# The last block's expert outputs 4 and 5: weighed by ScalarE and added by GpSimd instead of VectorE, with expert 5's matmuls moved earlier on TensorE

## What is computed

```python
x = x + _L0_xattn_ref(_layernorm(x), ctx, mask, ...)      # 16 heads over 77 context rows, with a mask
x = x + _L0_ffn_ref(_layernorm(x), proj_w, anchors, ...)  # 6 experts, the 2 best weighed by a softmax
x = x + _L1_xattn_ref(_layernorm(x), ctx, ctx, ...)       # 16 heads, one key and value head
x = x + _L1_ffn_ref(_layernorm(x), w1, b1, w2, b2)        # 256 -> 1024 -> 256, piecewise gelu
```

```python
h = jax.nn.gelu(jnp.einsum('btd,edh->bteh', x, w1))
out = jnp.einsum('bteh,ehd,bte->btd', h, w2, expert_weights)
```

## Time and profile before

| | us |
|---|---|
| median of 3 executions (793.67 to 794.06) | 793.94 |
| the profiled execution, whole | 797.73 |
| its span, first to last instruction | 795.5 |
| TensorE busy (93% of the span) | 736.2 |
| VectorE busy (82%) | 648.8 |
| ScalarE busy (65%) | 514.5 |
| GpSimd busy (47%) | 371.8 |

### The profile page before, as it was taken

One profiled execution on the slowest core, in us unless ns is written; L12 is line 12 of the kernel. 1 busy time (PEld: TensorE's weight loads), 2 busy tenths in 40 slices (PEclk: granted clock), 3 DMA queues, 4 the chain that ended last, 5 costly groups with the idle time before them and its releaser, 6 DMA issues. The chain is left out here.

```text
span 795.5 us, 13555 instructions
## 1 busy us (share of the span) xinstructions
PE 736.2 (93%) x4372; PEld 552.0 (69%) x4372; DVE 648.8 (82%) x1546; ACT 514.5 (65%) x943; POOL 371.8 (47%) x323
## 2 busy tenths in 40 slices
PE   4799999999999999999989999999869999999995
PEld 3465666666558888888865555555448898888985
DVE  7647777787877878888887888988687999999995
ACT  3545655565654456545536777777677889898985
POOL 6473444334122223233214232232157899999985
PEclk9989999999999999999998999999998999999999
DMA  7985535653310000001057666755000000000001
GB/s 230 133 201 113 131 73 111 119 115 80 77 35 1 1 1 7 1 1 54 1 70 118 83 81 82 134 77 78 13 1 1 2 27 28 28 27 2 27 28 53
DMA packets 25102, 48.64 MB, mean 61 GB/s; under 512 B 3687, under 2 KB 7017, under 8 KB 24521
## 3 DMA queue, kind: packets, MB, share of 16 engines
q1 hardware_dynamic: 23366, 46.54, 30.5%
q10 hardware_dynamic: 1666, 1.24, 0.5%
HBM read 12.12 MB, written 4.19 MB: 21 GB/s over the span
## 5 line engine op out<-in xcount | busy, mean ns | idle before, releaser
L316 ACT ACTIVATE pt<-bank 77x512 f32<-77x512 f32 x256 | 140.8, 589 | 82.7 <-PE bank L416 60.0
L342 DVE TENSOR_REDUCE mx<-bank 128x4 f32<-128x308 f32 x256 | 108.7, 471 | 22.8 <-PE bank L391 12.2
L413 PE MATMUL bank<-qst,l_kst 128*77 128x512 f32 (+1 forms) x256 | 103.2, 418 | 17.0 <-DMA qst<-mt 11.0
L720 POOL TENSOR_TENSOR frise<-fg,fg 128x512 f32<-128x512 f32 x64 | 100.3, 1568 | 6.8 <-ACT fg L738 1.2
L388 PE MATMUL bank<-l_kblk,qh 128*128 128x308 f32 x256 | 81.0, 334 | 7.7 <-DVE mx L342 6.3
L284 POOL TENSOR_TENSOR ol<-ot,oh 128x512 fp32r<-128x512 f32 x32 | 41.4, 1292 | 98.1 <-ACT oh L321 54.6
L617 DVE SCALAR_TENSOR_TENSOR x<-bank,eweight,x 128x256 f32<-128x256 f32 x192 | 79.6, 477 | 4.6 <-PE bank L649 4.3
L103 POOL TENSOR_TENSOR rstd<-var,minus_half 128x4 f32<-128x4 f32 x32 | 34.8, 1088 | 102.7 <-DVE var L98 53.9
L413 PEld LDWEIGHTS bank<-qst,l_kst 128*77 128x77 f32 (+1 forms) x256 | 36.6, 146 | 66.5 <-ACT pt L316 24.8
L811 PE MATMUL bank<-fw2h,fyh 128*128 128x256 f32 x256 | 73.6, 288 | 5.4 <-DVE fyl L779 5.3
L114 ACT ACTIVATE xn<-x,shift,rstd 128x256 f32<-128x256 f32 (+1 forms) x128 | 67.0, 592 | 17.0 <-POOL shift L105 17.0
(11 more groups left out here) (176 smaller groups left out, 2101.1 us busy)
## 6 DMA issues: line engine op xcount, KB each, us to landing
qst<-qh SPq DMA_DIRECT2D x64, 256.0 KB, 6.6
qst<-ql SPq DMA_DIRECT2D x32, 256.0 KB, 9.0
out<-x SPq DMA_DIRECT2D x8, 512.0 KB, 2.6
qst<-ml SPq DMA_DIRECT2D x8, 480.0 KB
x<-in_x SPq DMA_DIRECT2D x3, 1024.0 KB, 12.9
weights<-in_mlp_w SPq DMA_DIRECT2D x2, 1024.0 KB, 5.1
mraw<-in_mask SPq DMA_DIRECT2D x8, 154.0 KB
x<-in_x SPq DMA_DIRECT2D x2, 512.0 KB, 5.5
```

The costliest lines, as they stand in the source:

```text
L316: self.nc.scalar.activation(self.pt[0:T, i // 4 % 2, i % 4, :], self.bank_of(G, i)[0:T, :], ACT.Exp).then_inc(self.probs, 1)
L342: self.nc.vector.reduce_max(out, banks[u % len(banks)][:, 0:4 * T].rearrange("q (p par t) -> q p par t", p=2, par=2), AX.X).then_inc(self. ...
L413: last = self.nc.tensor.matmul(out, layer.kst[rows, layer.stack(c * HC + 2 * k + par), b * T:(b + 1) * T], self.qst[rows, self.slot(G), c ...
L720: self.nc.gpsimd.tensor_tensor(self.rise[:, k % 2, :], self.g1[:, k % self.R, :], self.g0[:, k % self.R, :], ALU.subtract).then_inc(self.r ...
```

## The change

The weighted outputs of experts 4 and 5 of the last block no longer pass through VectorE. ScalarE copies the banks, multiplied by the router's weight, into a new SBUF tile `epart` (`scale_last`: 4 instructions of 128x256 for each expert), and GpSimd adds `epart` to `x` (`add_last`: 2 instructions of 128x512 for each expert). `output` of expert 5 waits for `scaled` instead of `added`, and stands on TensorE between units 5 and 6 of block 8 instead of behind `turn_maxima`. Whoever waited for the last `added` now waits for `last_added` (GpSimd's adds) or, for the bank alone, for `scaled`. The core of the diff:

```diff
+ALL_EXP = 2 * (E * BLOCKS - 2)
...
+        self.part = place.at("epart", m["epart"], [P, 2, NT, D], F32)
...
+    def add_last(self, pool, i):
+
+        pool.wait_ge(self.added, ALL_EXP)
+        start = (BLOCKS - 1) * NT
+        for k in range(2):
+            pool.wait_ge(self.scaled, 2 * i + k + 1)
+            tiles = self.norm.x[:, start + 2 * k:start + 2 * k + 2, :]
+            self.nc.gpsimd.tensor_tensor(tiles, tiles, self.part[:, i, 2 * k:2 * k + 2, :], ALU.add).then_inc(self.last_added, 1)
+            pool.wait_ge(self.last_added, 2 * i + k + 1)
...
+    def scale_last(self, act, i):
+
+        g, e = BLOCKS - 1, 4 + i
+        act.wait_ge(self.weight_ready, BLOCKS)
+        for k in range(2):
+            act.wait_ge(self.out_done, 2 * (E * g + e) + k + 1)
+            for t in range(2):
+                last = self.nc.scalar.activation(self.part[:, i, 2 * k + t, :], self.OUT[k][:, t * D:(t + 1) * D], ACT.Copy,
+                                                 scale=self.weight[:, g % 2, 2 * k + t, e:e + 1])
+            last.then_inc(self.scaled, 1)
...
     def output(self, pe, g, e):
         self.wait_rest(pe, g, e)
         for k in range(2):
-            need(pe, self.added, 2 * (E * g + e - 1) + k + 1)
+            if (g, e) == (BLOCKS - 1, E - 1):
+                pe.wait_ge(self.scaled, k + 1)
+            else:
+                need(pe, self.added, 2 * (E * g + e - 1) + k + 1)
...
                 att.stack_maxima(sp, BLOCKS)
-                sp.wait_ge(ex.added, ALL_EXP)
+                sp.wait_ge(ex.last_added, 4)
                 sp.dma_start(ff.row0[:], d["mlp_w1_0"].to_broadcast([P, F])).then_inc(ff.row0_in, 16)
...
-                pool.wait_ge(ex.added, ALL_EXP)
+                for i in range(2):
+                    ex.add_last(pool, i)
                 nc.gpsimd.memset(ff.bias2[:].bitcast(F32), 0.0).then_inc(ff.cleared, 1)
...
                 for c in range(C):
                     att.leading(act, BLOCKS, c)
+                ex.scale_last(act, 0)
                 norm.norm(act, LN_ATT1 + 1)
+                ex.scale_last(act, 1)
                 att.maxima(act, BLOCKS, FIRST_MAX1[0])
...
                 att.take_maxima(dve, BLOCKS, range(4, 16), FIRST_MAX1)
-                for e in (4, 5):
-                    ex.add(dve, BLOCKS - 1, e)
                 for c in range(C):
                     norm.rest(dve, LN_ATT1 + 1, c, att.W[c], att.xh, att.xl)
...
                 for u in range(16):
+                    if u == 6:
+                        ex.output(pe, BLOCKS - 1, 5)
                     att.max_unit(pe, l1, BLOCKS, u, FIRST_MAX1)
                 att.turn_maxima(pe, BLOCKS, FIRST_MAX1[0])
-                ex.output(pe, BLOCKS - 1, 5)
...
                         if G == BLOCKS and i == 1:
-                            pe.wait_ge(ex.added, ALL_EXP)
+                            pe.wait_ge(ex.scaled, 4)
```

More of the change, by code:

```diff
@@ L502, in __init__ @@
         self.added = sem("eadded")
+        self.scaled = sem("escaled")
+        self.last_added = sem("elast_added")
         self.chain = 0
@@ L827, in memory_map @@
               "id5": z + 68608, "klowf": z + 70176, "rows": z + 70816, "ones_row": z + 72864, "id5f": z + 73184})
-    m.update({"ew1h": z, "ew1l": z + 6144, "ew2raw": z + 12288, "exh0": z + 47616, "exl0": z + 51712, "ehh": z + 19712,
+    m.update({"ew1h": z, "ew1l": z + 6144, "ew2raw": z + 12288, "exh0": z + 47616, "epart": z + 47616, "exl0": z + 51712, "ehh": z + 19712,
               "ehl": z + 25856, "eq": z + 12288, "router": z + 70176, "exh1": z + 39424, "exl1": z + 43520,
@@ L887, in build @@
         wh1_ready, wl1_ready = sem("wh1_ready"), sem("wl1_ready")
-        ALL_EXP = 2 * E * BLOCKS
         UNITS1 = {1: (0,), 2: (1,), 3: (2,), 4: (3,), 5: (4, 5), 6: (6, 7), 7: (8, 9), 9: (10,), 10: (11,), 11: (14, 15)}
@@ L1239, in _ @@
                                 act.wait_ge(ff.shifted, 2)
-                                act.wait_ge(ex.added, ALL_EXP)
+                                act.wait_ge(ex.last_added, 4)
                             part = (slice(None), k // 2, slice(512 * (k % 2), 512 * (k % 2) + 512))
@@ L1395, in _ @@
                     p, n, nm = G - 1, G + 1, LN_ATT1 + G - BLOCKS + 2
-                    if nm < LN_FFN:
+                    if nm == LN_FFN - 1:
+                        dve.wait_ge(ex.last_added, 4)
+                    elif nm < LN_FFN:
                         dve.wait_ge(ex.added, 2 * E * (nm - LN_ATT1 + 1))
```

## The result

The changed kernel takes 795.41 us (median of 20 executions, 793.71 to 799.36), the kernel before 793.88 (20 executions, 792.59 to 794.62). The ratio is 1.0025 with a 95% interval of 1.0016 to 1.0033: slower by 1.3 to 2.6 us. (The ratio weighs all executions; the two medians alone are 1.53 us apart.) The profiled execution took 796.09 us, its span is 794.3 us. Two later executions of the kernel before, beside kernels 10 to 12, took 900 and 1010 us at granted clocks of 0.75 and 0.65 and are left out of the comparisons.

The account below looks back on a forecast made before the run. Two chains bound the seam: `mt`'s landing for score 0, and block 9's queries. 0.1 (`frow`) - 0.25 (queries earlier) + 1.6 (half clock) = +1.45, less 0.1 absorbed, +1.35 us: 795.3 us, range 793.5 to 796.6.

Parts of the forecast that it names:

- the half clock lasts longer: Rival at block 9's queries: clock still low 4.5 us after score 0, +2.1 to +2.6 us, 796.2 us, chance 0.3.
- the signs named in advance: Score 0 within 0.3 us; gap over 3 us; clock near 0.5; queries 0.43 us apart; unit 0, `mt` 1 to 2 later.
- Score 0 is bound by the landing of `mt`: Block 8's score 0 waits for `mt` behind DMA traffic; `mt` could be issued about 1.5 us later without moving it.
- the queue: The six copies of block 8's queries stand ahead of `mt`, DMA engines full until 418.3 (share 1.05).
- Expert 5's output hides between the units: Behind unit 5 at full clock it takes 1.4 us; maxima 0 to 0.3 us late, 0.1 taken, covered: 0.
- ScalarE's copies and GpSimd's adds cost nothing: Eight copies of 0.45 us and four adds of 1289 ns at the seam are hidden: 0.
- `frow` right behind `mt`: 0.1 us: SyncE issues the 512 KB load right behind `mt`; worth 0 to 0.12 us by block 12's row, 0.1 taken.
- Queries start earlier: 0.25 us: Block 9's queries wait for scores 0 and 1 alone, starting at 422.45 instead of 422.70: gain 0.25 us.
- Half clock: 1.6 us, between 1.5 and 2.8: After a TensorE gap of 3.2 to 4.3 us, scores 0, 1 and part of block 9's queries run at half clock.
- my longer case: Clock back only after 6.0 us, all 14 matmuls from score 0 on at half clock: 2.8 us.
- 0.1 us is absorbed later: Behind unit 0 of block 9, small waits that fill up take 0.1 us off the +1.45 us, leaving +1.35.
- the second rule: Transposes do not count as busy like matmuls, so TensorE would be idle for the clock from the last unit on.

Follow-up runs that it names:

- kernel 10: kernel 3 with SyncE issuing block 8's maxima ahead of the last of the six query copies; 791.52 us, ratio to before 0.9978.
- kernel 11: the kernel before with the maxima issued ahead of the last of the six query copies, nothing else changed; 793.60 us, ratio to before 0.9997.
- kernel 12: the changed kernel with the small loads held back and the maxima issued ahead of the last query copy; 793.58 us, ratio to before 1.0004.
- kernel 3: the changed kernel with expert 5's output behind block 9's transposes, ScalarE's last four weighted copies behind `xh`; 793.35 us, ratio to before 0.9998.
- kernel 2: the changed kernel with the small loads `frow`, `frows` held back until scores 0 and 1 of block 8; 794.45 us, ratio to before 1.0015.
- kernel 8: kernel 3 with block 8's maxima sent from ScalarE's DMA queue instead of SyncE's; 793.36 us, ratio to before 0.9999.
- kernel 1: the changed kernel with 16 extra unread matmuls between block 9's transposes and score 0; 793.64 us, ratio to before 1.0006.
- kernel 4: the changed kernel with expert 5's output back behind the turned maxima, ScalarE's last four copies behind `mt`; 792.24 us, ratio to before 0.9992.
- kernel 5: the kernel before with expert 5's 12 matmuls and 4 adds of the last block left out; 795.65 us, ratio to before 1.0035.
- kernel 9: the changed kernel with 8 extra matmuls ahead of score 0 and the small loads held back; 793.39 us, ratio to before 1.0003.

## Why the prediction was right, and where its sizes were off

The predicted 795.3 us stands against 795.41. The mechanism is the one forecast: the queries behind a longer wait lost the full clock. That the number fits so closely is in part luck. The sum was 1.35 us and the medians are 1.53 apart, but the profiled seam is 2.94 us longer, beyond the forecast's own 0.9 to 1.8. In that profile the half clock lasts from score 0 at 420.20 to about 425.8, longer than the 4.5 us at which the prediction had its first rival, "the half clock lasts longer", decide. Of the signs named in advance the gap of over 3 us, the clock near 0.5, the 0.43 us between queries and the delay of block 9's `mt` came; two did not: score 0 is 0.68 us later and not within 0.3, unit 0 is 2.94 us later and not 1 to 2.

- *Score 0 is bound by the landing of `mt`.* Right: against kernels 3 and 2, kernels 10 and 12 move it by the order of the copies alone. That `mt` waits behind full DMA engines is right too, but "the queue" was too narrow: kernel 8.
- *Expert 5's output hides between the units.* Right: 1.49 us for 1.4; the twelve reductions take 4.90 us instead of 4.71, 0.2 us late where I took 0.1. What the sum did not have: with these matmuls between the units the turned maxima run at full clock, 0.60 us instead of 1.02, so `mt` is issued 0.23 us earlier (7.73 for 7.96). So they do in five of the six profiles with the output there (not in kernel 1's), and in none of the seven with it elsewhere or left out.
- *ScalarE's copies and GpSimd's adds cost nothing.* Right, by kernel 4; 480 ns where I took 450, and 1280 for 1289.
- *`frow` right behind `mt`: 0.1 us.* Mis-sized. It is 0.6 us (kernel 2). The row of block 12 that bounded it had empty DMA engines (share 0.07 in 497.90 to 498.90), the seam has full ones (1.06 in 410.00 to 414.80).
- *Queries start earlier: 0.25 us.* Small: 0.4 us counted to unit 0 (3.63 to 3.23).
- *Half clock: 1.6 us, between 1.5 and 2.8.* In profiles 2.66 (changed), 2.74 (kernel 2), 1.93 (kernel 5) and 1.59 (kernel 12). The profile of the changed kernel met my longer case. The turned maxima and transposes ran at full clock there, so the gap was longer than the 3.2 to 4.3 us forecast.
- *0.1 us is absorbed later.* Nothing is up to the last block of this stage: 2.93 of 2.94 us arrive at block 9's `mt`, and block 15's, issued at 561.11 against 560.50, is 3.02 us later from unit 4. Behind it the two profiles part for another reason, told below.

By the terms of the profile the loss is 2.9 us, by the ratio 1.3 to 2.6. The executions of the changed kernel spread over 5.7 us where those of before spread over 2.0 beside it (over 3.0 to 3.9 beside the other kernels); the four slowest, 797.1 to 799.4 us, are those with the lowest granted clock over the whole kernel, 0.984, the three fastest have 0.989. Yet the profiled one, 796.09 us with twelve queries at half clock, has the highest of all, 0.991: that mean takes in other places too. So that the half clock costs a different number of matmuls in each execution, and that one profile is one draw of it, is likely but not shown for this seam. It is shown for another place, where none of the edits lies, the wait on the way to the last stage. In the changed kernel:

```profile
597.22 1.12 PE L128 MATMUL bank<-ident,xn 128*128 128x128 f32 x4 [2.96 <-DVE fxl L137]
```

Behind this wait of 2.96 us the clock was at half for some 6 us before and some 3 in the changed kernel and kernels 1 and 2, and stayed at 1.00 in kernels 4, 5, 8 and 10 (the same transposes take 0.66 us there). From block 15's `mt` to the next store of `x` the changed kernel's profile takes 76.14 us and that of before 77.61.

My chances (0.53 for no difference, 0.40 for slower) put too much on the first: the interval lies on both sides of the 0.2% that I had named, with its middle above it.

Left open is which waits cost the clock. Where it was at full ahead of the gap, it stayed so through 2.75 us (kernel 9) and fell in or right behind 3.42, 4.56 and 5.13 us (kernels 12 and 2, the changed one); 1.86 and 2.96 us at two other places lost it in the profile before, while the clock stayed full through 2.23 us at the first place in the changed kernel's profile and through 2.96 us at the second in kernel 4's. Whether transposes count as activity, which the second rule weighed in the prediction says they do not in the same way (the Trainium skill, "TensorE: Matmul & The Clock Gate", Part 4), no run here separates. Of kernel 10's 3.70 us between issue and score 0, 0.76 more than block 9's 2.94, the cause was not tried; the copy of 256 KB issued 0.75 us behind `mt`, as `frow` was, is a candidate.

## What to carry to other kernels

Before work is moved off a stretch in which TensorE waits for a transfer, look at what runs right behind the wait: if those are matmuls on the critical chain, the work may be what gives them the full clock, and the move can cost more than it frees. Independent matmuls belonged close ahead of the wait's end here (kernels 3 and 4), not as early as they could go. When a small transfer gates a chain, issue the large ones that nobody needs yet behind it, and not right behind it while the DMA engines are full; changing the order did more here than changing the queue.

## What the runs showed of the hardware that was not expected

A transfer of 512 KB issued 0.73 us behind one of 32 KB delays the earlier one's landing by 0.6 us when six copies of 256 KB are still draining (5.36 against 4.78 us to score 0), while 1 MB issued 0.69 us behind it on idle engines made the step 0.12 us longer. Sending the small one from another engine's queue shortened its way by 0.26 us only (4.65 to 4.39), moving one 256 KB copy from ahead of it to behind it by 0.95 us (4.65 to 3.70). One and the same wait of 2.96 us cost TensorE's clock in four profiles and did not in four others. And a kernel from which 12 matmuls and 4 vector adds are taken is slower by 0.35% (0.21 to 0.50).
